# The first expert stage of a one-core hybrid kernel, split into three quarters and one quarter of the tokens

## Chip, core and metric

The kernel runs on one core of one Trainium2 chip. The metric is the device time of one execution in microseconds, as the median of several runs. TensorE (PE), VectorE (DVE), ScalarE (ACT) and GpSimd (POOL) each execute their own instructions in order and meet through semaphores; SyncE (SP) issues the transfers. A wait holds up everything that is queued behind it on its engine.

## What is computed

The input is 8 images of 64 channels and 16 x 16 pixels. Two convolution blocks are followed by four residual stages on 2048 tokens of 64 channels (`_ln_t` is a layer norm without weights):

```python
t = t + _L2_attn_ref(_ln_t(t), ...)   # softmax attention, 8 heads of 64
t = t + _L2_ffn_ref(_ln_t(t), ...)    # 8 experts, hidden 128, gelu, two chosen per token
t = t + _L3_attn_ref(_ln_t(t), ...)   # attention with a pseudo-inverse of W_Q as key weights
t = t + _L3_ffn_ref(_ln_t(t), ...)    # 16 experts, hidden 128, silu, two chosen per token
```

In `_L2_ffn_ref` the gates are a softmax over 8 logits of which the two largest per token are kept; every expert is computed for every token, its hidden layer is multiplied by the gate, and the outputs and gated biases are summed.

## The kernel before

**Stages.** The order is: convolutions, first norm, attention of L2, second norm with gates, first expert stage, third norm, attention of L3, fourth norm with gates, second expert stage. The 2048 tokens are 16 tiles of 128, or 4 chunks of 512. Attention round j (4 of them) covers images 2j and 2j+1, which are the 4 tiles of chunk j. `T` is the residual stream, `XS` the normalised stream turned to channels, split into a high part (rounded for the fast fp32r products) and the low rest.

**Attention.** A round has 8 pairs of heads. `attention_steps` (L335) runs each engine's `step(j, k)`, software-pipelined: four steps ahead, a hardware loop over rounds 0 to 2 with 8 steps each (k = 2 to 9), then the 8 steps of the last round written out. In one step DVE takes row maxima (`maxima`, L1574), splits keys (L1566), inverts row sums (L1581) and copies turned probabilities (L603); ACT does the exponentials (L619), key copies (L610), one turned copy (L601) and value copies; POOL scales the probabilities (`scale_rows`, L504) twice, for rows 2k+2 and 2k+3; PE makes scores (L857), keys (L833, L834), transposes (`turn`, L868), products (L884) and, every fourth step, `value` and `turn_out` (L895). `add_out` (L1589) adds a finished half round to `T`.

**Newton.** Inside the loop each step also has one Newton iteration for the pseudo-inverse: POOL makes `nsZ` (`newton_z`, L512) as its first instruction of the step; DVE makes `nsY` from it (`newton_y`, L1602) between the two maxima; PE uses `nsY` (L909, L910) after `turn(2k+1)`; DVE copies back (L1607). The order on DVE in a step is written out:

```python
maxima(j, 2 * k + 2)
newton_y(j, k - 2)          # in the loop; waits for POOL's nsZ
key_low(j, k + 2)
invert_sums(j, 2 * k + 2)
maxima(j, 2 * k + 3)        # then add_out in some steps
newton_x(j, k - 2)
transposed_copy(dve, j, 2 * k + 1)
invert_sums(j, 2 * k + 3)
```

**Second norm and gates.** After the attention, `layer_norm(1)` on DVE (L1504 statistics, L1508 to L1514 moments, L1522 scaling) works with POOL's centring of half the tiles (L462), ACT's square root (L574, with table loads), PE's transposes (L794), ACT's high parts (L369) and DVE's low parts (L377). `start_sums` (L954) puts the stream into the PSUM banks of the sums. `gate_pe` (L807) makes logits, `gate(0)` on DVE chooses (L1536 to L1542), ACT takes exponentials (L584) and loads the Gelu table (L586), DVE makes the gates (L1544 to L1549), PE turns them (L818) and ACT copies them into `gT` (L590). SP stores `gT` to HBM (L432) and loads it back as one row per expert, spread over 128 partitions (L441): 512 KB per half row, two per expert, in three buffers that are used in turn.

**First expert stage.** Items kk = 0 to 31 are (expert, chunk) with the chunk running fastest. PE makes a hidden item (L968, two fp32r matmuls of 512 columns), ACT the gelu (L725), DVE the multiplication by the gate row (L1650), PE the output matmul (`output`, L976, fp32, 64 output channels), which adds to one half of the partitions of bank 6 or 7: chunks 0 and 1 to the two halves of bank 6, chunks 2 and 3 to those of bank 7. A ring of 16 hidden items lies between; PE makes 16 hidden items, then 8 outputs, 8 hidden, 8 outputs, 8 hidden, 16 outputs. `biases` (L996) adds the gated biases. During the stage POOL splits the weights of the second expert stage into high and low parts (`split_weights`, L454 and L456, four experts at a time). ACT's copy of bank 6 (L741) ends the stage.

Of the kernel before, what the change touches and what calls it, by code (L numbers as in the profile page):

```python
# [21 lines left out]
F32 = mybir.dt.float32  # L22
# [6 lines left out]
P = 128  # L29
# [11 lines left out]
RING, GROUP = 16, 8  # L41
CT = CHUNK // P
# [7 lines left out]
NEWTON = (J - 1) * PAIRS  # L50
HIDDEN_SCORE = -30000.0
# [89 lines left out]
def hybrid_kernel(nc, io, out):  # L141
    ctx = ExitStack()
    with ctx:
# [33 lines left out]
        def from_early(rows, words):  # L177
# [65 lines left out]
                  for s in range(2))  # L243
# [43 lines left out]
                     over(at_keys, "gate_row_keys", [P, TOK])[:]]  # L287
        hid_more = sb("hid_more", [P, 2, CHUNK])
# [41 lines left out]
        def gate_slot(which, e):  # L330

            so_far = sum(f % 3 == e % 3 for f in range(EXP2)) if which == 3 else 0
            return e % 3, so_far + e // 3 + 1

        def attention_steps(eng, step, in_loop=None):  # L335
# [13 lines left out]
            for k in range(2, 2 + PAIRS):  # L349
                step(J - 1, k, lambda pair: pair < PAIRS)  # L350

# [12 lines left out]

        def split_high(act, stack, bank, p, signal):
# [6 lines left out]
        def split_low(dve, stack, bank, p, high, so_far, signal):  # L372

            for odd in range(2):
                h, o = slice(C * odd, C * odd + C), slice(C * (1 - odd), C * (1 - odd) + C)
                dve.wait_ge(S(high), so_far + 2 * p + odd + 1)
# [9 lines left out]
        def _(sp):  # L386
# [42 lines left out]
            for which, experts, rows in ((2, EXP2, gates_row2), (3, EXP3, gates_row3)):  # L429
                sp.wait_ge(S("gT_ready"), 2 * (which - 1))  # L430
                for o in range(2):
                    sp.dma_start(rows.rearrange("e (q o n) -> o e q n", o=2, n=P)[o],  # L432
                                 gT[C * o:C * o + experts]).then_inc(S("gates_stored"), 16)
                sp.wait_ge(S("gates_stored"), 32 * (which - 1))
                for e in range(experts):
                    slot, _ = gate_slot(which, e)
                    if e >= 3:
                        sp.wait_ge(S(f"f{which}_hid_ready"), CHUNKS * (e - 2))
                    for half in range(2):
                        at = slice(half * TOK // 2, (half + 1) * TOK // 2)  # L440
                        sp.dma_start(gate_rows[slot][:, at], rows[e:e + 1, at].broadcast_to([P, TOK // 2])).then_inc(  # L441
                            S(f"gate_row{slot}_{half}"), 16)
# [16 lines left out]
        def ln_pool(gp, n):  # L459

            gp.wait_ge(S("ln_mean"), n + 1)
# [37 lines left out]
        def attention_pool(gp):  # L499
# [14 lines left out]

            def step(j, k, there):
                if not isinstance(j, int):
                    newton_z(j, k - 2)
                if there(k + 1):
                    scale_rows(j, 2 * k + 2)
                    scale_rows(j, 2 * k + 3)  # L520

            gp.wait_ge(S("consts_loaded"), 16)
            attention_steps(gp, step)

        @block.gpsimd
        def _(gp):
# [5 lines left out]
            gp.memset(zeros[:], 0.0).then_inc(S("zeros_ready"), 1)  # L532
            gp.wait_ge(S("zeros_ready"), 1)
# [8 lines left out]
            gp.wait_ge(S("ln_normalised"), 4)  # L542
# [5 lines left out]
            ln_pool(gp, 1)  # L548
            gp.wait_ge(S("gates_ready"), 1)
            split_weights(gp, w3hl, w3raw, [slice(e, e + 4) for e in range(0, EXP3, 4)], "w3_loaded", "w3_high", "w3_split")  # L550
            ln_pool(gp, 2)
            l3_pool(gp)
            ln_pool(gp, 3)

            for kk in range(CHUNKS * EXP3):
                e, c = kk // CHUNKS, kk % CHUNKS
                slot, filled = gate_slot(3, e)
                gp.wait_ge(S(f"gate_row{slot}_{c // 2}"), 16 * filled)
# [12 lines left out]
        def ln_act(act, n, table_after=None):  # L571

            act.wait_ge(S("ln_var"), n + 1)
            act.activation(lnc[:, 6, :], lnc[:, 5, :], ACT.Sqrt).then_inc(S("ln_std"), 1)  # L574
            if table_after:
                act.preload_act_table(table_after)
            for p in range(4):
                act.wait_ge(S("ln_transposed"), 4 * n + p + 1)
                split_high(act, XS, p, p, "ln_high")
# [1176 lines left out]
```

## Time and profile before

| | us |
|---|---|
| median of 3 runs (lowest, highest) | 418.89 (418.32, 419.47) |
| the profiled execution | 416.06 |
| its span, first to last instruction | 414.3 |
| granted TensorE clock, mean over the span | 0.897 of full speed |
| busy: PE, DVE, ACT, POOL | 350.9, 283.2, 217.5, 189.2 |

Times inside the profile count from the start of the span. The attention loop runs to about 182, its last round to 206.9, the norm and gates to 218.4, and the first expert stage to about 262. A row of the timeline shows start, duration, engine, line and operation; "x8" means that eight such instructions are merged, and the bracket gives the engine's idle time just before and who ended it.

### The profile page before, as it was taken

To read this page: it belongs to the slowest core of one execution; us is meant where nothing else is said; L and a number is where in the kernel's file an instruction comes from. 1 tells how busy PE (TensorE), PEld (TensorE's weight loads), DVE (VectorE), ACT (ScalarE), POOL (GpSimd) and SP (SyncE) were. 2 spreads that over 40 slices of the span, in tenths; PEclk is the share of its full clock that TensorE was granted. 3 is DMA by queue.
4 is the path that set the end of the run, shared out by engine and by line. 5 is a ranking of instruction groups with operands and counts; after the bars stand their busy time and mean duration, and the time that the engine had idled before them with its cause. 6 is when DMAs were issued, how large, how long until landed. Compare 5 with 4: busy or idle time off the path is not lost.

```text
span 414.3 us, 6910 instructions
## 1 busy us (share of the span) xinstructions
PE 350.9 (85%) x2145; PEld 246.1 (59%) x2147; DVE 283.2 (68%) x689; ACT 217.5 (52%) x541; POOL 189.2 (46%) x186
## 2 busy tenths in 40 slices
PE   5666259999999999999769699877258999999996
PEld 1552156787888878887467244374147756666662
DVE  2767876788878878877493587579798545555441
ACT  0534258677677767778547435261315634444441
POOL 4120025545454545545315800122110299999994
PEclk9867559999999999999977789968556999999999
DMA  6916000000000000000000795000000576666521
GB/s 185 235 21 205 0 0 1 2 2 2 2 0 0 0 0 0 0 0 2 1 2 5 288 329 197 2 0 2 1 0 2 193 273 215 222 208 224 204 101 52
DMA packets 17002, 32.87 MB, mean 79 GB/s; under 512 B 6032, under 2 KB 9808, under 8 KB 16976
## 3 DMA queue, kind: packets, MB, share of 16 engines
q1 hardware_dynamic: 16976, 32.55, 23.9%
q8 instruction: 13, 0.21, 0.2%
q14 instruction: 13, 0.11, 0.1%
HBM read 31.83 MB, written 0.72 MB: 79 GB/s over the span
## 4 chain that ended last, share of the span: by engine, by line
PE 61%; DVE 19%; ACT 9%; issue 6%; DMA 3%; POOL 1%; SPq 0%; DVEq 0%; ACTq 0%; POOLq 0%
PE ps L1020 14%; PE ps L1028 7%; PE ps L857 6%; PE ps L884 5%; PE ps L868 5%; PE ps L976 4%; ACT va_vb L619 4%; DVE ln L1504 2%; DVE negmax L1574 2%; PE ps L968 2%; PE ps L807 2%; DMA pT<-gates_row 1%; PE ps L910 1%; PE ps L834 1%; PE ps L833 1%
## 5 line engine op out<-in xcount | busy, mean ns | idle before, releaser
L504 POOL TENSOR_TENSOR va_vb<-va_vb,rowinv 128x512 f32<-128x512 f32 x64 | 67.2, 1050 | 72.1 <-DVE rowinv L1581 72.1
L619 ACT ACTIVATE va_vb<-ps,negmax 128x256 f32<-128x256 f32 x128 | 59.5, 472 | 11.2 <-DVE negmax L1574 10.9
L1020 PE MATMUL ps<-XS,w3hl 128*128 128x512 f32 x256 | 63.4, 406 | 0.7 <-ACT gT L590 0.7
L733 ACT ACTIVATE wy<-ps 128x512 f32<-128x512 f32 x64 | 38.2, 598 | 45.6 <-PE ps L1020 45.6
L1020 PEld LDWEIGHTS ps<-XS,w3hl 128*128 128x128 f32 x256 | 48.6, 193 | 17.2 <-issue 4.9
L1574 DVE TENSOR_REDUCE negmax<-ps 128x2 f32<-128x512 f32 x64 | 44.0, 688 | 7.8 <-PE ps L857 5.6
L857 PE MATMUL ps<-keys_gates,xcur 128*128 128x256 f32 x256 | 47.4, 308 | 2.2 <-DVE keys_gates L1566 2.2
L857 PEld LDWEIGHTS ps<-keys_gates,xcur 128*128 128x128 f32 x256 | 35.1, 193 | 14.8 <-issue 11.5
L868 PE MATMUL ps<-consts,va_vb 128*128 128x128 f32 x256 | 39.5, 277 | 4.2 <-POOL va_vb L504 2.4
L462 POOL TENSOR_TENSOR xn<-T,lnc 128x512 f32<-128x512 f32 x4 | 4.2, 1042 | 74.0 <-DVE lnc L1512 74.0
L868 PEld LDWEIGHTS ps<-consts,va_vb 128*128 128x128 f32 x256 | 29.7, 147 | 9.8 <-POOL va_vb L504 4.8
L884 PE MATMUL ps<-pT,vproj 128*64 128x256 f32 x256 | 34.5, 392 | 0.0
L610 ACT ACTIVATE keys_gates<-ps 128x512 fp32r<-128x512 f32 x32 | 19.2, 600 | 25.8 <-PE ps L834 25.5
L619 ACT ACTIVATION_READ_ACCUMULATOR va_vb<-ps,negmax 128x1 f32 x128 | 25.7, 201 | 0.0
L603 DVE COPY pT<-ps 128x512 f32<-128x512 f32 x32 | 21.8, 681 | 1.9 <-PE ps L868 1.9
L1566 DVE TENSOR_TENSOR keys_gates<-ps,keys_gates 128x512 fp32r<-128x512 f32 x32 | 21.8, 683 | 1.4 <-ACT keys_gates L610 1.4
L1667 DVE TENSOR_TENSOR theta_qk<-ps,wy 128x512 f32<-128x512 f32 x16 | 11.1, 692 | 15.3 <-ACT wy L733 15.3
L884 PEld LDWEIGHTS ps<-pT,vproj 128*64 128x64 f32 x256 | 15.6, 136 | 8.9 <-issue 1.4
L601 ACT ACTIVATE pT<-ps 128x512 f32<-128x512 f32 x32 | 19.2, 601 | 0.2 <-PE ps L868 0.2
L1581 DVE RECIPROCAL rowinv<-rowsum 128x2 f32<-128x2 f32 x64 | 10.6, 165 | 12.7 <-ACT va_vb L619 10.7
L968 PE MATMUL ps<-XS,w2hl 128*128 128x512 f32 x64 | 18.6, 444 | 0.2 <-ACT x L725 0.2
L833 PE MATMUL ps<-xcur,AH 128*128 128x256 f32 x64 | 17.4, 293 | 0.5 <-DVE xcur L1559 0.5
(323 smaller groups left out, 727.9 us busy)
## 6 DMA issues: line engine op xcount, KB each, us to landing
pT<-gates_row SPq DMA_DIRECT2D x18, 512.0 KB, 4.8
vproj<-gates_row SPq DMA_DIRECT2D x16, 512.0 KB, 5.4
gate_row_keys<-gates_row SPq DMA_DIRECT2D x14, 512.0 KB, 4.9
early<-in_f_in SPq DMA_DIRECT2D x1, 2048.0 KB, 8.8
consts<-in_consts SPq DMA_DIRECT2D x1, 816.0 KB, 4.9
x<-in_x SPq DMA_DIRECT2D x1, 512.0 KB, 3.7
w2raw<-in_f_in SPq DMA_DIRECT2D x1, 512.0 KB, 3.5
out<-in_f_out SPq DMA_DIRECT2D x1, 512.0 KB
```

The costliest lines, as they stand in the source:

```text
L504: gp.tensor_tensor(prob[:, n % 4], prob[:, n % 4], rowinv[:, n % 4, :].unsqueeze(2).broadcast_to([P, U, N]), ALU.mult).then_inc(S("p_scale ...
L603: eng.tensor_copy(dst, src).then_inc(S("pT_odd"), 1)
L619: ins = act.activation(prob[:, n % 4, u, :], ps[:, 1 + n % 2, u * N:(u + 1) * N], ACT.Exp, bias=negmax[:, n % 4, u:u + 1], accum_out=rowsu ...
L733: act.activation(act_out[:, kk % 2, :], ps[:, 2 * (kk % 3), :], ACT.Silu).then_inc(S("f3_act"), 1)
L857: mm = pe.matmul(ps[:, 1 + n % 2, u * N:(u + 1) * N], xcur[:, g, u * P:(u + 1) * P], K[:, k % 2, n % 2, :], start=(part == 0), stop=(part ...
L868: mm = pe.transpose(ps[:, 3 + n % 2, su * N + u * P:su * N + (u + 1) * P], prob[:, n % 4, u, su * P:(su + 1) * P], ident)
L884: mm = pe.matmul(ps[h * C:(h + 1) * C, 5, 0:N], vproj[:, g, su, head * C:(head + 1) * C], pT[:, (2 * k + h) % 4, su, :], start=(k % 4 == 0 ...
L968: mm = pe.matmul(ps[:, kk % 4, :], w2hl[:, s, e], XS[:, c * CHUNK:(c + 1) * CHUNK], start=(s == 0), stop=(s == 1))
L1020: mm = pe.matmul(ps[:, 2 * (kk % 3) + w, :], w3hl[:, s, e, w * HID:(w + 1) * HID], XS[:, c * CHUNK:(c + 1) * CHUNK], start=(s == 0), stop= ...
L1028: pe.matmul(ps[half, bank, :], out3[:, e, :], hid[kk % RING], start=False, stop=False, skip_group_check=True).then_inc(S("f3_out_chunk"), 1)
L1566: tt(KL[:, k % 2].rearrange("p h n -> p (h n)"), ps[:, 0, :], KH[:, k % 2].rearrange("p h n -> p (h n)").bitcast(F32), ALU.subtract).then_ ...
L1574: dve.tensor_reduce(negmax[:, n % 4, :], ps[:, 1 + n % 2, :].rearrange("p (u n) -> p u n", u=U), AX.X, ALU.max, negate=True).then_inc(S("m ...
```

## The change

Layer norm n = 1 covers chunks 0 to 2 and is done in pieces behind the steps of the last attention round; a new norm n = 2 covers chunk 3 and is done inside the first expert stage. The norms are numbered 0 to 4 from here on. Cut to its core:

```diff
+NORMS = [(0, 1, 2, 3), (0, 1, 2), (3,), (0, 1, 2, 3), (0, 1, 2, 3)]
+SPLIT_A_ROUND = EXP3 // (J - 1)
+early_chunks = [(e, c) for e in range(EXP2) for c in NORMS[1]]
+first_experts = early_chunks + [(e, c) for e in range(EXP2) for c in NORMS[2]]
 def attention_steps(eng, step, in_loop=None, behind=lambda k: None):
             for k in range(2, 2 + PAIRS):
                 step(J - 1, k, lambda pair: pair < PAIRS)
+                behind(k)
```

POOL, attention (256 elements a partition are split for one expert; `split_weights` of w3 and `ln_pool(1)` behind the attention are gone):

```diff
             def step(j, k, there):
...
                     newton_z(j, k - 2)
+                i = k - 4
+                so_far = j * SPLIT_A_ROUND + i if in_loop else EXP3 - 1
+                splits = (in_loop and 0 <= i < SPLIT_A_ROUND) or (not in_loop and j == J - 1 and k == 2)
                 if there(k + 1):
                     scale_rows(j, 2 * k + 2)
+                    if splits:
+                        split_high_of(expert)
+                        gp.wait_ge(S("w3_high"), so_far + 1)
                     scale_rows(j, 2 * k + 3)
+                    if splits:
+                        split_low_of(expert)
```

Behind the steps of the last round, on DVE, ACT and PE (on PE `between(k)` stands inside the step, ahead of `turn(2k+1)`):

```diff
+                if k == 2:                                   # DVE
+                    split_pinv()
+                    dve.wait_ge(S("stream_added"), G + G * (J - 1))
+                    stats(1)
+                if k == 3:
+                    moments(1)
+                    centre(1, NORMS[1])
+                if k == 4:
+                    scale(1)
+                if k in (5, 6, 7):
+                    low(1, k - 5, 6)
+                if k == 9:
+                    choose(0, EXP2, gb2, [(tiles_of_norm(1), 6, 0)])
...
+                if k == 3:                                   # ACT
+                    ln_root(act, 1, ACT.Exp)
+                if k in (5, 6, 7):
+                    ln_highs(act, 1, lambda i: 6, (k - 5,))
+                if k == 9:
+                    gate_exp(act, 0, EXP2, tiles_of_norm(1))
...
+            def between(k):                                  # PE
+                if k == 2: pinv product
+                if k in (5, 6, 7):
+                    pe.wait_ge(S("ln_low"), chunks_before(1) + k - 5)
+                    ln_turn(pe, 1, k - 5, 6)
+            def behind(k):
+                if k == 8:
+                    pe.wait_ge(S("ln_low"), chunks_before(2))
+                    gate_products(pe, 1, range(0, 12), 6, EXP2, gw2)
```

After the attention. DVE: `share_out(0)`, then stats, moments, centre, scale and low parts of norm 2, `weigh(0)`, `weigh(1)`, `choose(1)`, `weigh(2)`, `weigh(3)`, `share_out(1)`, `weigh(4)` and on. ACT and PE:

```diff
+            turned_gates(act, slice(0, 4), 4, 0)
+            turned_gates(act, slice(4, 6), 6, 1)
+            ln_root(act, 2, ACT.Gelu)
+            gelu 0, 1
+            ln_highs(act, 2, lambda i: 4, (0,))
+            gelu 2 to 7
+            gate_exp(act, 1, EXP2, tiles_of_norm(2), ACT.Gelu)
+            gelu 8 to 11
+            turned_gates(act, slice(6, 8), 4, 2)
+            gelu 12 and on
...
+            gates_turn(pe, range(0, 4), 4); gates_turn(pe, range(4, 6), 6)
+            hidden 0 to 3, ln_turn(pe, 2, 0, 4), start_sums, hidden 4 to 7
+            gate_products(pe, 2, range(12, 16), 5, EXP2, gw2)
+            biases(NORMS[1], 0), hidden 8 to 15
             for k in range(0, CHUNKS * EXP2, GROUP):
                 for kk in range(k, k + GROUP):
                     output(kk)
+                    if kk == 1:
+                        pe.wait_ge(S("gates_ready"), 2)
+                        gates_turn(pe, range(6, 8), 4)
+                if k + RING == len(early_chunks):
+                    pe.wait_ge(S("gT_ready"), 3)
+                    biases(NORMS[2], 1)
```

SP now loads a gate row in pieces of one chunk (256 KB each). The 24 early pieces have blocks of their own (`row_blocks`), so none waits for another; the 8 late ones reuse the first blocks:

```diff
+            sp.wait_ge(S("gT_ready"), 2)
+            store_gates(gates_row2, EXP2, slice(0, 6), 0)
+            for e in range(EXP2):
+                if e == 3:
+                    sp.wait_ge(S("pv_done"), PAIRS + J * PAIRS)
+                for c in NORMS[1]:
+                    first_row(early_row(e, c), e, c, f"first_gates{e}")
+            sp.wait_ge(S("gT_ready"), 3)
+            store_gates(gates_row2, EXP2, slice(6, 8), 32)
+            for e in range(EXP2):
+                sp.wait_ge(S("f2_hid_ready"), len(NORMS[1]) * (e + 1))
+                first_row(late_row(e), e, NORMS[2][0], f"first_gates{e}")
```

The item order of the first expert stage becomes chunks 0, 1, 2 of each expert (24 items), then chunk 3 of each (8 items). The later stages keep their work; only semaphore counts change there.

## Rows read from the trace of the kernel before

**Rows 1.** Stretches: us, busy (count) of PE, PEld, DVE, ACT, POOL; PE clock, DMA share, GB/s.
```profile
145.50:182.30 36.80, 36.29 (x291) 29.94 (x290) 29.79 (x69) 26.89 (x86) 18.96 (x25) 1.00 0.00 0
182.30:206.90 24.60, 22.28 (x170) 16.54 (x169) 14.69 (x32) 17.91 (x55) 11.16 (x11) 1.00 0.01 1
...
218.40:232.80 14.40, 11.97 (x43) 7.95 (x41) 3.47 (x17) 11.94 (x20) 10.74 (x7) 0.83 0.20 71
232.80:262.60 29.80, 28.63 (x114) 11.86 (x114) 21.77 (x32) 10.07 (x17) 3.50 (x2) 0.89 0.69 250
```

**Rows 2.** Timeline of one step of the attention loop, DVE and POOL.
```profile
169.88 0.35 DVE L1602 SCALAR_TENSOR_TENSOR nsY<-ps,nscoef,nsZ 128x128 f32<-128x128 f32 x1 [0.60 <-POOL nsZ L512]
...
172.58 0.17 DVE L1581 RECIPROCAL rowinv<-rowsum 128x2 f32<-128x2 f32 x1
...
172.82 1.04 POOL L504 TENSOR_TENSOR va_vb<-va_vb,rowinv 128x512 f32<-128x512 f32 x1 [0.80 <-DVE rowinv L1581]
...
173.82 0.29 POOL L512 TENSOR_TENSOR nsZ<-consts,nscoef 128x64 f32<-128x64 f32 x1
...
174.15 0.35 DVE L1602 SCALAR_TENSOR_TENSOR nsY<-ps,nscoef,nsZ 128x128 f32<-128x128 f32 x1 [0.26 <-POOL nsZ L512]
```

**Rows 3.** Timeline of DVE: newton_y in steps k = 4 and k = 9 of that round.
```profile
156.29 0.35 DVE L1602 SCALAR_TENSOR_TENSOR nsY<-ps,nscoef,nsZ 128x128 f32<-128x128 f32 x1 [0.35 <-POOL nsZ L512]
...
178.83 0.35 DVE L1602 SCALAR_TENSOR_TENSOR nsY<-ps,nscoef,nsZ 128x128 f32<-128x128 f32 x1 [0.35 <-POOL nsZ L512]
```

**Rows 4.** Waits, 112 to 145: engine, for whom, us in total, times, longest.
```profile
DVE nsY L1602 <- POOL nsZ L512: 2.9, 7, 0.7
```

**Rows 5.** POOL's groups by shape: busy, mean ns, then idle before.
```profile
L560 POOL TENSOR_TENSOR theta_qk<-theta_qk,gate_row_keys 128x512 f32<-128x512 f32 x8 | 10.1, 1304 | 0.4 <-DVE theta_qk L1667 0.4
...
L456 POOL TENSOR_TENSOR w3hl<-early,w3hl 128x1024 fp32r<-128x1024 f32 x4 | 9.8, 2450 | 0.3
...
L454 POOL CAST w3hl<-early 128x1024 fp32r<-128x1024 f32 x4 | 4.6, 1157 | 10.3 <-DVE gates L1549 10.3
```

**Rows 6.** Timeline of the last round's end: the last copy of turned probabilities.
```profile
203.53 0.69 DVE L603 COPY pT<-ps 128x512 f32<-128x512 f32 x1 [1.87 <-PE ps L868]
```

**Rows 7.** Timeline of the second norm and the gates.
```profile
207.41 2.11 DVE L1504 BATCH_NORM_STATS2 ln<-T 128x6 f32<-128x64 f32 x16
...
207.64 2.54 PE L954 MATMUL ps<-consts,T 128*64 128x128 f32 x32 [0.74 <-DVE qkvw L1639]
...
211.77 1.28 ACT L576 ACT_TABLE_LOAD   x1
...
212.42 1.43 DVE L1522 TENSOR_TENSOR xn<-xn,lnc 128x256 f32<-128x256 f32 x4
...
213.88 3.52 DVE L377 TENSOR_TENSOR XS<-ps,XS 64x256 fp32r<-64x256 f32 x8
...
214.88 3.60 PE L807 MATMUL ps<-gw,XS 128*64 128x8 f32 x64
...
217.69 0.64 DVE L1539 MAX8 top<-logit 128x8 f32<-128x8 f32 x8
```

**Rows 8.** Timeline of the first expert stage: store of the gates, first gated item, end.
```profile
225.23 1.56 SPq L432 DMA_DIRECT2D gates_row<-gT  x2
...
231.90 2.28 DVE L1650 TENSOR_TENSOR hid_al<-hid_al,pT 128x512 f32<-128x512 f32 x2 [10.15 <-DMA pT<-gates_row]
...
261.72 0.60 ACT L741 ACTIVATE x<-ps 128x512 f32<-128x512 f32 x1 [4.71 <-PE ps L976]
```

**Rows 9.** Timeline of PE: hidden and output items at full clock; a full-width fp32 product.
```profile
243.99 3.99 PE L968 MATMUL ps<-XS,w2hl 128*128 128x512 f32 x16
...
258.90 1.89 PE L976 MATMUL ps<-theta_qk,out 128*64 128x512 f32 x8
...
285.24 1.88 PE L1068 MATMUL ps<-f_prob,consts 128*128 128x512 f32 x4
```

**Rows 10.** A stretch of the expert stage: PE clock, DMA share and GB/s come last.
```profile
244.00:248.00 4.00, 4.00 (x20) 2.93 (x20) 3.17 (x6) 3.23 (x6) 0.00 (x0) 1.00 1.03 372
```

More of the change, by code:

```diff
@@ L330, in gate_slot, with early_row, late_row, attention_steps @@
         def gate_slot(which, e):
-            so_far = sum(f % 3 == e % 3 for f in range(EXP2)) if which == 3 else 0
-            return e % 3, so_far + e // 3 + 1
-        def attention_steps(eng, step, in_loop=None):
+            return e % 3, e // 3 + 1
+        def early_row(e, c):
+            return row_blocks[len(NORMS[1]) * e + c]
+        def late_row(e):
+            return row_blocks[e]
+        def attention_steps(eng, step, in_loop=None, behind=lambda k: None):
             for k in range(-2, 2):
@@ L823, in attention_pe, with gates_turn @@
+        def gates_turn(pe, pairs, bank):
+            for t in pairs:
+                at = (t - pairs[0]) * P
+                mm = pe.transpose(ps[:, bank, at:at + P], gates[:, 2 * t:2 * t + 2].rearrange("p t c -> p (t c)"), ident)
+            mm.then_inc(S("gates_transposed"), 1)
         def attention_pe(pe):
@@ L936, in step @@
                     upto(pe, "nsy_ready", j, PAIRS, k)
+                if not in_loop and j == J - 1:
+                    between(k)
                 if there(k):
@@ L1216, in _ @@
             start_sums(pe)
-            ln_pe(pe, 3)
-            gate_pe(pe, 1)
+            ln_pe(pe, 4)
+            for half in range(2):
+                gate_products(pe, 4, range(8 * half, 8 * half + 8), 4 + half, EXP3, gw3)
             ffn3_pe(pe)
@@ new lines, in centre, with scale @@
+            def centre(n, chunks):
+                for p in chunks:
+                    q = slice(CT * p, CT * p + CT)
+                    ins = tt(xn[:, q], T[:, q], wide(lnc[:, 1, q], t=CT), ALU.subtract)
+                step(ins)
+            def scale(n):
+                tiles = tiles_of_norm(n)
+                dve.wait_ge(S("ln_std"), n + 1)
+                step(dve.reciprocal(lnc[:, 7, tiles], lnc[:, 6, tiles]))
+                for p in NORMS[n]:
+                    q = slice(CT * p, CT * p + CT)
+                    if p == 2 and n in WHOLE:
+                        dve.wait_ge(S("ln_centred"), WHOLE.index(n) + 1)
+                    tt(xn[:, q], xn[:, q], wide(lnc[:, 7, q], t=CT), ALU.mult).then_inc(S("ln_normalised"), 1)
@@ new lines, in choose @@
+                tiles = slice(parts[0][0].start, parts[-1][0].stop)
+                count = tiles.stop - tiles.start
+                lg, gs = logit[:, tiles, 0:experts], gsel[:, tiles, 0:experts]
+                for k, (piece, bank, so_far) in enumerate(parts):
+                    dve.wait_ge(S("gate_logits"), so_far + 1)
+                    t = piece.stop - piece.start
+                    raw = ps[:, bank, 0:t * experts].rearrange("p (t e) -> p t e", e=experts)
+                    step(tt(logit[:, piece, 0:experts], raw, gb[:].unsqueeze(1).broadcast_to([P, t, experts]), ALU.add))
+                    for q in range(piece.start, piece.stop):
+                        ins = dve.max(top8[:, q, :], logit[:, q, 0:experts])
@@ L1652, in _ @@
+            stats(2)
+            moments(2)
+            centre(2, NORMS[2])
+            scale(2)
+            low(2, 0, 4)
+            for kk in range(2):
+                weigh(kk)
+            choose(1, EXP2, gb2, [(tiles_of_norm(2), 5, 1)])
+            for kk in range(2, 4):
+                weigh(kk)
+            share_out(1, EXP2, tiles_of_norm(2))
+            for kk in range(4, CHUNKS * EXP2):
+                weigh(kk)
             dve.wait_ge(S("f2_out_chunk"), CHUNKS * EXP2)
```

328 lines of the change are left out of this document (179 added, 149 removed).

## The prediction

> **What bounds the kernel now.** I read the stretches first [rows 1], to see which engine is short where. In a loop round (36.8 us, [rows 1]) PE is busy for 36.3, so it looks like the bound; POOL is busy for 19.0 and looks half free. In the last round PE is at 22.3 of 24.6 and DVE and ACT have 9.9 and 6.7 us idle. From 207.4 to 218.5 the norm and the logits run one after another [rows 7], and up to 232.8 DVE has almost nothing to do: it waits for the first gate row, which starts as a store at 225.23 and lets DVE go at 231.90 [rows 8]. From there to 261.72 PE is the bound again (28.6 busy in 29.8, [rows 1]). So the idle stretch between 206.9 and 231.9 is what the change goes for.
>
> Busy shares don't show a second bound in the loop. I read the waits [rows 4]: in every one of seven steps DVE waits for POOL's nsZ ahead of newton_y. One step [rows 2] shows the ring: newton_y at 169.88; DVE then works its queue down to the second reciprocal at 172.58 (2.70); POOL scales at 172.82; nsZ follows at 173.82 in the same queue; newton_y again at 174.15 (1.57). That is 4.27 us, the shortest step of the round. From step 4 to step 9 newton_y comes every (178.83 - 156.29) / 5 = 4.51 us [rows 3], and each time DVE has stood waiting for nsZ. PE's own pace is 36.3 / 8 = 4.5 us a step. Ring and PE are equally long.
>
> **The loop: 15 splits.** In steps k = 4 to 8 of each round POOL gets a cast and a subtraction of 256 elements. The subtraction takes 2.45 us at 1024 elements, a like one (two full operands) 1.30 at 512 [rows 5]: the slope is 1.15 / 512, so 256 elements cost 1.30 - 0.57 = 0.73, and about 0.78 if I take the undisturbed part of the slope; I take 0.78. The cast takes 1.16 at 1024 [rows 5], I estimate 0.35 at 256. It and its semaphore wait stand between the two scalings, where POOL idles for 0.80 [rows 2], so they cost nothing; without that gap they would cost 0.4 each. The subtraction stands behind the second scaling and ahead of the next step's nsZ, that is, in the ring. Everything behind newton_y on DVE (key split, reciprocals, second maximum, PSUM copy) waits for it, and with those ACT's exponentials, POOL's scaling and PE's transposes.
>
> A ring with it is at least 2.70 + 1.57 + 0.78 = 5.05 and at most 4.51 + 0.78 = 5.29 against the 4.51 of just these five steps now [rows 3]. Fifteen times 0.54 is 8.1, fifteen times 0.78 is 11.7, with some 0.8 on top for register work on the expert's address. No row shows an instruction with such an address on POOL. I take **+10 us**, bounds 8 and 12.5. The sixteenth split, in step 2 of the last round, has no nsZ behind it and is free.
>
> **The last round.** Each insertion is queued behind a step and ahead of the next step's first maximum (DVE) or key copy (ACT).
> - k = 2: the inverse's split, about 0.5, and 12 statistics, 12/16 of 2.11 [rows 7] = 1.6. DVE +2.1.
> - k = 3: moments, about 1.1 (an estimate: 2.25 lie between the end of the statistics and the table load at 211.77, [rows 7], with POOL's centring of 1.04 and the root of 0.2 among them), and three centrings at 1.43 / 4 = 0.36. DVE +2.2. ACT has two table loads of 1.28 and a root of 0.2: +2.8. The longer counts, and ACT's key copy is late next.
> - k = 4: reciprocal and three scalings, 1.35.
> - k = 5, 6, 7: per chunk two low parts of 0.44 [rows 7] on DVE and two high parts of about 0.4 on ACT, 0.9 and 0.8, side by side, shifted by one part; PE's transposes 0.5. PE's wait for the low parts of the chunk before stands ahead of turn(2k+1), where it holds up the products once the round is short of work. About 0.9, 0.4 and 0.3.
>
> The sum is 2.1 + 2.8 + 1.35 + 1.6 = 7.9. The idle time of the round absorbs little, since DVE's gaps are waits for ACT's exponentials and for PE, which move along. I take **+7.5** at the last copy of turned probabilities (203.53, [rows 6], to 211.0); bounds +3 (DVE's 14.7 us plus 9.5 of insertions just fit into 24.6) and +9.
>
> **From there to the first gated item.** Products follow the copy and now end at about 213. Ahead of turn_out PE has 48 of the 64 logit matmuls, 3.60 x 48/64 = 2.7 at half clock [rows 7], 1.5 at full: 214.9. Turn_out 0.5, add_out 0.3, choice of 12 tiles (12 x 0.08 from [rows 7], and three small ones, 1.8), exponential with latency 0.4, share_out 1.2, six transposes 1.2: hidden items start at 220.3, against 218.5 behind the logits [rows 7], later than now. But gT is ready at 221.1 instead of 225.23, since no norm and no Gelu table load is ahead. The same 6.7 us from store to first use [rows 8] and 0.6 for a third piece give the first gated item at **228.4 instead of 231.9**. That the rows come in pieces of 256 KB costs nothing as long as the DMA engines are full; 24 pieces, 6.3 MB at 372 GB/s [rows 10], land by about 243, ahead of the items.
>
> **From there to the end.** PE has 32 outputs (8 records in 1.72 us of spacing, so 0.43 an output, [rows 9]; 14), 16 hidden (3.92 for 8, [rows 9]; 7.8), bits of 1.0. That is 22.8. On top comes a new wait: behind output(1) PE waits for the second gates, which need ACT's exponential, queued behind gelu(7) and between two table loads of 1.28. ACT reaches it at about 231 and DVE shares out by 234: PE stands still for some 5 us, and weigh(4) and on with it. 228.4 + 22.8 + 5.2 = 256.4, against 262.4 now (261.72 with its last copy). The late rows queue behind the early ones on SP's ring and land by 252; the items want them then, so they cost 0 to 3. Also gone is POOL's splitting beside DVE's first multiplications (1.14 each in [rows 8], later ones about 0.65), which is in these numbers. Tail without the loop: **-6 us**, bounds -10 and -2.
>
> **The sum.** +10 - 6 = +4. The profiled execution's 416.06 becomes 420.1; it lies 2.8 below the median of the runs, so I put +4 on the median: 418.89 + 4 = **422.9**. Everything behind the stage is unchanged.
>
> **Rivals.**
> - *POOL's half-idle time covers the splits* (the side of faster). If nsZ has slack, the loop costs 1 us or less and the change gives 418.9 - 6 + 1 = 413.9. For it speaks POOL's 19.0 of 36.8 [rows 1]; against it [rows 2 to 4]: DVE stands waiting for nsZ in each step. It decides from where less than 0.4 of the 0.78 reaches newton_y. Chance 0.17.
> - *The order of the halves.* Outputs of 64 channels alternate between partition halves now. In the new order chunks 0, 2 and the next 0 share a half, and all eight late ones do. An fp32 product of full width needs 1.71 for four records of 512 columns, the 64-wide outputs 1.72 for eight [rows 9]: they may run two at a time because the halves differ. Then 8 pairs of records in the early part and 8 in the late part lose their partner, 16 x 0.43 = 6.9, and the time is 422.9 + 6.9 = 429.8. Against it: start_sums has eight records in a row on one half, and 32 of 128 columns take 2.54 [rows 7], 0.073 each; two cycles a column would be 0.107. So narrow fp32 products seem fast in either order, and the sum has nothing for it. The Trainium skill ("TensorE: Matmul & The Clock Gate", Part 3, packing small matmuls) says that small products run concurrently when they lie in distinct column groups, which is this rival's rule; by it the sum would be 429.8, and the start_sums row speaks against needing it. Chance 0.12.
> - *The tail pays for the loop.* The last round takes the insertions for +4 or the second gates cost no stall, while the loop is as forecast: tail -10, result 418.9. DVE's 9.9 idle us [rows 1] speak for it; that they are waits in a chain speaks against. Chance 0.14.
> - Forecast: 0.57.
>
> **The numbers.** 0.3% (1.26 us) is about what a measurement of this kernel can tell from no change. Forecast with its bounds: loop 8 to 12.5, tail -8 to -3, so 418.9 to 428.4, its own range. The range 414.5 to 430 reaches to the tail case and the halves and leaves the covered case mostly out. Slower: 0.52 + 0.12 + 0.03 = 0.67; same: 0.04 + 0.06 = 0.10; faster: 0.17 + 0.01 + 0.05 = 0.23.
>
> **What the profile will show.** Loop rounds of 40 us instead of 36.8, with DVE's wait for nsZ at 1 us or more in five of eight steps and PE no longer full; if rounds stay at 36.8, the ring was read wrongly. A last round of about 32 instead of 24.6, the root's table loads in its middle. First gated item 3.5 us earlier relative to the loop's end; PE waiting 5 us behind output(1). Outputs still at 0.43 each; at 0.6 or more in the early part, the halves decide.

## Result and profile after

| | before | after |
|---|---|---|
| median, us (lowest, highest) | 419.18 (418.32, 419.5) | 427.92 (426.92, 428.83) |
| profiled execution; span | 416.06; 414.3 | 427.19; 425.4 |
| last nsZ of the loop starts | 178.50 | 186.99 |
| last scaling of POOL starts | 201.74 | 217.91 |
| first gated item starts | 231.90 | 235.95 |
| statistics of the norm behind the first expert stage start | 264.74 | 275.10 |

The change makes the kernel slower by 8.7 us between the medians (a ratio of 1.021); the ratio of all its runs to those of before is on record as 1.0225, with a 95% interval of 1.0192 to 1.0259. The forecast was 4 us slower. (The median of before has one run more behind it here than in the table ahead of the prediction.) The two profiled executions are 11.1 us apart, because that of before lies 3.1 under its median and that of after only 0.7; 10.4 of these are there at the end of the first expert stage, which the next norm's statistics mark. I follow the time from one milestone to the next.

**The loop.** The page of after has a new kind of entry in its part 4, the chain that ended last: POOL's split of the late weights.

```profile
PE 41%; issue 21%; DVE 18%; POOL 9%; ACT 8%; DMA 1%; POOLq 1%; DVEq 0%; ACTq 0%; SPq 0%
PE ps L1138 12%; PE ps L1146 6%; PE ps L1085 5%; PE ps L1077 4%; ACT va_vb L689 3%; POOL va_vb L553 3%; POOL w3hl L568 3%; DVE ln L1622 2%; DVE negmax L1722 2%; DVE XS L406 2%; POOL nsZ L561 2%; POOL w3hl L565 1%; PE ps L1231 1%; PE ps L903 1%; DVE xn L1654 1%
```

POOL's timeline shows one step of it (L553 scales, L565 is the cast to the high part, L568 the subtraction that gives the low part, L561 nsZ):

```profile
144.16 1.04 POOL L553 TENSOR_TENSOR va_vb<-va_vb,rowinv 128x512 f32<-128x512 f32 x1 [1.13 <-DVE rowinv L1729]
145.15 0.40 POOL L565 CAST w3hl<-early  x1
146.01 1.13 POOL L553 TENSOR_TENSOR va_vb<-va_vb,rowinv 128x512 f32<-128x512 f32 x1 [0.46 <-DVE rowinv L1729]
147.10 0.74 POOL L568 TENSOR_TENSOR w3hl<-early,w3hl  x1
147.79 0.30 POOL L561 TENSOR_TENSOR nsZ<-consts,nscoef 128x64 f32<-128x64 f32 x1
```

nsZ starts at 142.73 and again at 147.79: 5.06 us for a step with a split. The subtraction stands between the second scaling and nsZ, and nsZ is what DVE waits for. The waits of DVE from 112 to 152 (for whom, us in total, times, longest) say the same, against 2.9 us in 7 times before [rows 4]:

```profile
DVE nsY L1750 <- POOL nsZ L561: 6.3, 7, 1.1
```

From the first nsZ to the last the loop now takes 112.5 us (74.50 to 186.99), where it took 104.9 (73.63 to 178.50). So the loop costs 7.6; the other 0.9 of the difference in the table is there before the first nsZ. Profiles of kernels that are the same up to that point put it anywhere from 73.6 to 75.7.

**The stretches** (columns as in [rows 1]): a piece of the loop, of the last round, the start of the expert items, and their end.

```profile
110.00:150.00 40.00, 38.03 (x296) 30.50 (x297) 29.69 (x72) 27.19 (x87) 24.84 (x35) 1.00 0.00 0
190.00:214.00 24.00, 19.39 (x136) 14.17 (x135) 19.07 (x56) 16.64 (x48) 10.29 (x11) 1.00 0.00 1
234.00:246.00 12.00, 11.94 (x71) 6.70 (x68) 9.50 (x25) 9.63 (x16) 0.00 (x0) 1.00 1.02 366
254.00:273.00 19.00, 18.94 (x66) 7.73 (x65) 6.39 (x12) 5.62 (x10) 0.00 (x0) 1.00 0.52 96
```

In these 24 us of the last round DVE is busy for 19.1, where it was at 14.7 of 24.6 [rows 1]: the insertions are there, and from the last nsZ to POOL's last scaling the round gets longer by 7.7 ((217.91 - 201.74) - (186.99 - 178.50)). In the last two rows PE hardly pauses and its granted clock is full; before, the stage had 0.89 [rows 1]. A stage with PE full at full clock that is still longer must have more PE time in it. The chain of waits shows where (start, us, what; PE is the chain all the way):

```profile
228.72 3.27 PE ps L1077 x8
...
232.20 2.50 PE ps L1063 x32
234.70 2.04 PE ps L1077 x8
236.74 0.57 PE ps L903 x16
237.31 1.02 PE ps L1096 x6
...
238.37 1.07 PE ps L1096 x6
239.45 4.44 PE ps L1077 x16
243.89 1.01 PE ps L1085 x4
244.90 0.37 PE ps L910 x2
245.27 3.58 PE ps L1085 x12
248.85 3.91 PE ps L1077 x16
252.76 5.29 PE ps L1085 x16
...
259.32 3.92 PE ps L1077 x16
263.25 9.66 PE ps L1085 x32
```

L1085 is the output product, two records for each. 32 records took 9.66 us here. In before's chain of waits the same piece is 7.07 long:

```profile
255.49 7.07 PE ps L976 x32
```

All 64 records together: 1.01 + 3.58 + 5.29 + 9.66 = 19.5 us, where 64 at the spacing of 1.72 / 8 [rows 9] would be 13.8. The first gated item starts at 235.95, the first output only at 243.82, with PE busy all the time between on what the new order put ahead of it: the rest of the hidden items 4 to 7 (L1077), the logits of the last tiles (L903), the gated biases (L1096), and the hidden items 8 to 15.

### The profile page after: what moved, and what is told of

It is laid out like the page before. It is cut to its first block, busy times and chain, and to the rows that moved or that the text cites. A ratio compares the mean times of both kernels' runs of the same rounds, so it can differ in the third digit from the quotient of the medians.

```text
span 425.4 us, 7015 instructions
## 1 busy us (share of the span) xinstructions
PE 356.6 (84%) x2147; PEld 245.4 (58%) x2147; DVE 280.9 (66%) x706; ACT 222.0 (52%) x547; POOL 190.0 (45%) x208
## 3 DMA queue, kind: packets, MB, share of 16 engines
q1 hardware_dynamic: 19296, 32.56, 24.6%
## 4 chain that ended last, share of the span: by engine, by line
PE 41%; issue 21%; DVE 18%; POOL 9%; ACT 8%; DMA 1%; POOLq 1%; DVEq 0%; ACTq 0%; SPq 0%
PE ps L1138 12%; PE ps L1146 6%; PE ps L1085 5%; PE ps L1077 4%; ACT va_vb L689 3%; POOL va_vb L553 3%; POOL w3hl L568 3%; DVE ln L1622 2%; DVE negmax L1722 2%; DVE XS L406 2%; POOL nsZ L561 2%; POOL w3hl L565 1%; PE ps L1231 1%; PE ps L903 1%; DVE xn L1654 1%
## 5 line engine op out<-in xcount | busy, mean ns | idle before, releaser
L553 POOL TENSOR_TENSOR va_vb<-va_vb,rowinv 128x512 f32<-128x512 f32 x64 | 67.2, 1050 | 70.9 <-DVE rowinv L1729 70.9
L511 POOL TENSOR_TENSOR xn<-T,lnc 128x512 f32<-128x512 f32 x3 | 3.1, 1042 | 94.3 <-DVE lnc L1632 94.3
L958 PEld LDWEIGHTS ps<-consts,va_vb 128*128 128x128 f32 x256 | 28.8, 146 | 17.2 <-DVE nsY L1750 11.5
L1850 DVE TENSOR_TENSOR theta_qk<-ps,wy 128x512 f32<-128x512 f32 x16 | 11.1, 692 | 15.3 <-ACT wy L810 15.3
L1750 DVE SCALAR_TENSOR_TENSOR nsY<-ps,nscoef,nsZ 128x128 f32<-128x128 f32 x24 | 8.4, 350 | 19.0 <-POOL nsZ L561 19.0
L1729 DVE RECIPROCAL rowinv<-rowsum 128x2 f32<-128x2 f32 x64 | 10.4, 163 | 12.6 <-ACT va_vb L689 11.8
L1077 PE MATMUL ps<-XS,w2hl 128*128 128x512 f32 x64 | 18.2, 437 | 0.0
```

The lines of the kernel that those rows point to most:

```text
L553: gp.tensor_tensor(prob[:, n % 4], prob[:, n % 4], rowinv[:, n % 4, :].unsqueeze(2).broadcast_to([P, U, N]), ALU.mult).then_inc(S("p_scale ...
L958: mm = pe.transpose(ps[:, 3 + n % 2, su * N + u * P:su * N + (u + 1) * P], prob[:, n % 4, u, su * P:(su + 1) * P], ident)
L1077: mm = pe.matmul(ps[:, kk % 4, :], w2hl[:, s, e], XS[:, c * CHUNK:(c + 1) * CHUNK], start=(s == 0), stop=(s == 1))
```

## Experiments

Four theories were left. **Ring**: the place of the subtraction costs the loop's part. **Halves**: outputs on one partition half in a row cost double. **Late rows**, against the second: the late gate rows set the end. **Table loads**: ACT's table loads cost what the last round lost.

### 1. The low split behind nsZ

```diff
                 if in_loop:
                     newton_z(j, k - 2)
+                if in_loop and 1 <= k - 4 <= SPLIT_A_ROUND:
+                    split_low_of(bass.ds(j * SPLIT_A_ROUND + k - 5, 1))
...
                     scale_rows(j, 2 * k + 3)
-                    if splits:
+                    if splits and not in_loop:
                         split_low_of(expert)
```

> The changed kernel, with the same 16 splits and one edit: in the loop the subtraction of an expert's low part stands behind the next step's nsZ instead of ahead of it. Ring theory (newton_y waits for nsZ, which waits for POOL's queue): steps go back from 5.0 to about 4.5 us, a loop round from 39.2 to about 36.8, the whole from 427.9 to about 420. Rival, the amount of POOL's work slows the loop (contention with DVE, more instructions), wherever it stands: rounds stay at 39.2 and the time at 427.9.

Measured: 420.96 us (418.76 to 421.81), ratio to before 1.0033 (1.001 to 1.0056), so 7.0 below after, as the ring theory expected. The last nsZ starts at 179.33 instead of 186.99, and from the first to the last there are 105.0 us, the 104.9 of before. POOL's timeline and DVE's wait from 108 to 145:

```profile
136.89 1.04 POOL L553 TENSOR_TENSOR va_vb<-va_vb,rowinv 128x512 f32<-128x512 f32 x1 [0.46 <-DVE rowinv L1731]
137.89 0.29 POOL L561 TENSOR_TENSOR nsZ<-consts,nscoef 128x64 f32<-128x64 f32 x1
138.14 0.74 POOL L568 TENSOR_TENSOR w3hl<-early,w3hl  x1
```

```profile
DVE nsY L1752 <- POOL nsZ L561: 2.9, 7, 0.7
```

The same fifteen splits, on the same engine, now cost the loop nothing: the wait is back at the 2.9 of before [rows 4]. From one nsZ to the next it is 142.56 - 137.89 = 4.67 here, against 5.06. The ring theory holds. It was never POOL's load, only what stood ahead of nsZ.

### 2. The items with alternating halves, alone and with experiment 1

```diff
-        first_experts = early_chunks + [(e, c) for e in range(EXP2) for c in NORMS[2]]
+        first_experts = [(e, c) for e in range(EXP2) for c in (0, 1)] + [(e, c) for e in range(EXP2) for c in (2, 3)]
```

SP's order of rows, their semaphores and two of the buffers follow.

> The changed kernel, with the first expert stage in another order of items: first chunks 0 and 1 of all experts, then chunks 2 and 3 of all, so that every output product lies on the other half of the partitions than the one before. Halves theory: an output costs 0.43 us instead of 0.43 to 0.86, the stage ends about 6.9 us earlier, 421.0. Rival, the late rows of chunk 3 set the end (they land at a lower rate than the early ones): the stage ends no earlier, since those rows come no earlier; 427 to 429.

> Both edits together. Ring and halves theories: the gains add, 427.9 - 8 - 6.9 = about 413, below the kernel before (419.2) by 6, which is the return of the earlier first gated item less the cost of the last round. If the two share a cause, they don't add: 420 or more.

Measured: 431.06 us (430.94 to 431.27), 3.1 above after; with experiment 1 423.84 (422.19 to 425.75), 2.9 above experiment 1 alone. Both expectations of a gain fail, and the total is even above the range of the rival, late rows (427 to 429). The timeline of PE shows both why it should have held and what took its place:

```profile
253.19 1.94 PE L1086 MATMUL ps<-theta_qk,out 128*64 128x512 f32 x8
254.96 1.89 PE L1086 MATMUL ps<-probT_rot,out 128*64 128x512 f32 x8
...
263.97 1.67 PE L1086 MATMUL ps<-hid_al,out 128*64 128x512 f32 x4 [1.95 <-DVE hid_al L1823]
265.67 1.67 PE L1086 MATMUL ps<-hid_g,out 128*64 128x512 f32 x4
```

The alternating outputs are back at 8 records in 1.77 us. The last sixteen, four records in 1.67, wait for the multiplication, and that waits for its gate row. Behind 264 the DMA engines are full and move little (last two columns, share and GB/s). The single rows also start late: the store of the second gates, which they need, takes 6.8 us to land behind the rows that are already under way (252.72 to 259.5 in the chain of waits; the first store took 1.6).

```profile
252.00:256.00 4.00, 4.00 (x20) 1.67 (x20) 0.00 (x0) 2.77 (x5) 0.00 (x0) 1.00 0.59 170
...
268.00:273.00 5.00, 4.92 (x14) 1.24 (x14) 3.88 (x6) 0.00 (x0) 0.00 (x0) 1.00 0.99 159
```

That is 159 GB/s at a share of 0.99, where [rows 10] has 372 at 1.03. Rows of a single chunk, one for each expert, lie 8 KB apart in DRAM. Whether that is the reason stayed open until experiment 7.

### 3. Before, with its chunks in the order 0, 2, 1, 3

```diff
-                e, c = kk // CHUNKS, kk % CHUNKS
+                e, c = kk // CHUNKS, (0, 2, 1, 3)[kk % CHUNKS]
```

The same in hidden, output and DVE's multiplication; ACT's last copy waits for one output more. The halves then come as 0, 0, 1, 1.

> The kernel before, with chunks of an expert in the order 0, 2, 1, 3, so that the halves of the partitions come as 0, 0, 1, 1 instead of 0, 1, 0, 1; everything else is the same. Halves theory: of 8 records of 4 outputs only two pairs overlap, 6 x 0.43 instead of 4 x 0.43 us, +0.86 for each of 8 experts: +6.9 less what is hidden early in the stage, 424 to 426. If narrow fp32 products run at the same rate in any order: 419.2.

Measured: 417.77 us (416.56 to 421.69), ratio 0.9987 (0.9953 to 1.0022): no difference. Its four runs at a mean clock of 0.89 or less, where most of before's are, take 420.7 to 421.7 against before's 418.8 to 420.9, so a small cost isn't excluded; the expected 5 to 7 us are. I had expected a loss, and this miss corrected the theory. The timeline of PE at the start of the last sixteen outputs, of which the first two read hid_al (one half) and the next two hid_g (the other); I call these four items 0 to 3:

```profile
257.39 0.64 PE L976 MATMUL ps<-hid_al,out 128*64 128x512 f32 x1
257.40 0.64 PE L976 MATMUL ps<-hid_g,out 128*64 128x512 f32 x1
257.87 0.59 PE L976 MATMUL ps<-hid_al,out 128*64 128x512 f32 x1
257.88 0.59 PE L976 MATMUL ps<-hid_g,out 128*64 128x512 f32 x1
```

Item 2's first record starts 0.01 us behind item 0's first and 0.47 ahead of item 0's second. PE fetched it past the second record of item 0 and all of item 1, which stand ahead of it in the program. (The text ahead of the prediction says that each engine executes its instructions in order; for these products of PE that doesn't hold.) The Trainium skill ("TensorE: Matmul & The Clock Gate", Part 3) calls matmuls strictly first in, first out; for products on different halves these starts say otherwise, and the measurement decides. So, within what PE can look ahead, what counts is not who is whose neighbour but how many outputs of a stretch lie on either half. In after these are 5 and 3, 6 and 2, and in the last sixteen 5 and 11. With 0.86 us for each on the fuller half (twice the 0.432 of experiment 4) that makes 4.3, 5.2 and 9.5; the chain has 4.59, 5.29 and 9.66.

### 4. Narrow products by themselves

A kernel that only multiplies; all of the reference's work is left out. 16 products of each kind follow one another:

```diff
+            for k in range(16):   # halves alternate
+                pe.matmul(half(k % 2, 2, 512), w(k, C), x0[:, 0:512], ...)
+            for k in range(16):   # one half
+                pe.matmul(half(0, 3, 512), w(k, C), x0[:, 0:512], ...)
+            for k in range(16):   # full width
+                pe.matmul(ps[:, 4, :], w(k, P), x0[:, 0:512], ...)
```

and the same at 256 and 128 columns, and with four on one half, then four on the other, as `start_sums` has them.

> Only products, in groups of 16 with nothing between: all the reference's work is left out. Spacing of the records tells how narrow fp32 products run. Halves theory: 64 output channels, 512 columns, alternating halves 0.21 us a record; the same half 0.43; full width 0.43. At 128 columns on the same half 0.11 would follow, where start_sums showed 0.073: if 128 columns on the same half come out at 0.07, the cost depends on the columns in another way than two cycles each.

```profile
17.65 7.09 PE L194 MATMUL ps<-x 128*64 128x512 f32 x32
24.56 13.90 PE L196 MATMUL ps<-x 128*64 128x512 f32 x32
38.39 14.00 PE L198 MATMUL ps<-x 128*128 128x512 f32 x32
...
67.97 3.66 PE L208 MATMUL ps<-consts,x 128*64 128x128 f32 x32
71.47 2.52 PE L210 MATMUL ps<-consts,x 128*64 128x128 f32 x32
73.91 3.84 PE L212 MATMUL ps<-x 128*128 128x128 f32 x32
```

The granted clock is full in all of these. From start to start, 512 columns cost 6.91 / 32 = 0.216 us a record on alternating halves (L194), 13.83 / 32 = 0.432 on one half (L196) and 0.435 at full width (L198). A product of half the width on one half saves nothing. At 128 columns one half costs 3.50 / 32 = 0.109 (L208), and four and four 2.44 / 32 = 0.076 (L210). The last is close to the number that my prediction read off `start_sums` (0.073) and took for the price of one half. It was the price of two halves at a time. The halves theory holds at 128 columns too.

### 5. Before, with only the splits moved into the loop, as the change has them and with the low split behind nsZ

```diff
+SPLIT_A_ROUND = EXP3 // (J - 1)
...
                     scale_rows(j, 2 * k + 2)
+                    if splits:
+                        split_high_of(expert)
+                        gp.wait_ge(S("w3_high"), so_far + 1)
                     scale_rows(j, 2 * k + 3)
+                    if splits:
+                        split_low_of(expert)
...
-            split_weights(gp, w3hl, w3raw, [slice(e, e + 4) for e in range(0, EXP3, 4)], "w3_loaded", "w3_high", "w3_split")
```

> The kernel before, with the splits of the second expert stage's weights moved into the attention loop as the change has them, and nothing else. Ring theory: the loop costs the 8 us that the changed kernel shows. Behind it POOL no longer splits beside DVE's first gated items, which gives back 1 to 2. Sum +6 to +8: 425 to 427. If the splits cost nothing in the loop: 417 to 418.

> The kernel of e5_before_loop_splits (before, with the splits of the last stage's weights moved into the attention loop) with one edit: the low split stands behind the next step's nsZ, as in e1. e5 took 421.42 with its last nsZ at 187.0 and the later stages about 6 us shorter than before's. If the ring theory holds here as in e1, the last nsZ falls to about 179.3 and the time to 421.4 - 7.0 = 414.4 (412.5 to 416.5), faster than before: then moving the splits is worth it, and only the place of the low split in POOL's step cost. If the time e5 got back later was won only because its attention came late (weights and rows waiting ready), it stays with the loop and the time is 418 to 420.

Measured: 421.42 us (419.89 to 425.39), ratio 1.0059 (1.0029 to 1.009), less than the 425 to 427 expected; with the low split behind nsZ 417.45 (414.38 to 420.26), ratio 0.9983 (0.9945 to 1.0021), not to be told from before and in neither of the two ranges expected. The last nsZ starts at 187.02 in the first, +8.5 as in after, and at 178.68 in the second. But the time falls by 4.0, or by 3.2 if each is taken against before on its own chip, and not by 7. From the first gated item to the next norm the first takes 29.7 us (241.2 to 270.9), the second 35.3 (232.3 to 267.5), and before 32.8. The granted clock is the third number from the end of these rows, which are first of the kernel with the low split behind nsZ, then of the other:

```profile
235.00:240.00 5.00, 4.17 (x13) 1.34 (x12) 4.74 (x8) 0.00 (x0) 0.00 (x0) 0.50 1.03 377
240.00:245.00 5.00, 4.93 (x18) 1.52 (x16) 4.08 (x7) 0.00 (x0) 0.00 (x0) 0.50 1.01 407
```

```profile
235.00:240.00 5.00, 3.93 (x14) 1.81 (x13) 0.00 (x0) 5.00 (x10) 0.00 (x0) 1.00 0.43 123
240.00:245.00 5.00, 3.09 (x7) 1.05 (x8) 3.04 (x5) 0.46 (x1) 0.00 (x0) 0.73 0.94 338
```

In the first pair PE multiplies its items at 0.50, that is at 1.2 GHz, for all of the ten microseconds; in the second mostly at 2.4 GHz, but its gated items only start at 241.2. Over the whole stage, from each kernel's first gated item to its next norm, the mean clock is 0.81 with the low split behind nsZ, 0.94 in the other, and 0.90 before. Part of what the late loop lost came back as clock. The runs say the same. At a mean clock of 0.91 over the whole kernel the first took 419.9 to 421.5, and the one run of the second at 0.909 took 414.4, about 7 less. The other nine runs of the second had 0.886 to 0.898 and took 415.9 to 420.3. (The profiled execution of the second is one of those, 2.6 above its median.) What moved the low stretch was not tested.

### 6. The insertions behind the last round; the root without table loads

The first moves every insertion of the last round behind it. The second takes a plain copy instead of the square root in norm 1, which leaves that root out, and its two table loads.

```diff
+            for k in range(2, 2 + PAIRS):
+                behind(k)
```

```diff
-            act.activation(lnc[:, 6, tiles], lnc[:, 5, tiles], ACT.Sqrt)
-            if table_after:
+            act.activation(lnc[:, 6, tiles], lnc[:, 5, tiles], ACT.Copy if n == 1 else ACT.Sqrt)
+            if table_after and n != 1:
```

> The changed kernel, with all pieces of norm 1, its turns, logits and choice done behind the last attention round instead of within it. If the insertions cost the last round 7.7 us and are cheap only because they lie within it, the round goes back to 24.6 us and the pieces then take about 12 us behind it in a row: +3 to +5, 431 to 433. If the pieces cost more within the round than behind it (each step waits for them on three engines): 427.9 or less.

> The changed kernel, with a copy in place of the square root of norm 1 and without its two table loads (the gates of the early tokens are thus other values; the work is the same otherwise). If ACT's two loads of 1.28 us in step 3 of the last round are on the path: -2 to -2.6 us, 425.5. If DVE's moments and centring beside them set that step: -0.6 at most.

Measured: 432.91 us (431.31 to 433.78) and 426.82 (425.79 to 427.9), so 5.0 above and 1.1 below after. The insertions are worth 5 us where the change put them, as expected. For the loads, 1.1 lies between the two expectations (2 to 2.6, or 0.6 at most), so I read the profiles. From the last nsZ to POOL's last scaling there are 216.67 - 186.06 = 30.61 us without the loads and 217.91 - 186.99 = 30.92 with them. The loads cost the round 0.3. Of the rest, 0.9 in these two profiles lies ahead of the last nsZ (186.06 and 186.99), where the two kernels are the same. So the table loads are not what makes the kernel slow, and DVE's share of the step alone fills nearly all of its place.

### 7. The gate rows 10 KB apart

One edit on three kernels: experiment 1 with 2, experiment 2 alone, and the changed kernel. The store writes the same 8 KB of each row as before.

```diff
-        gates_row2 = nc.dram_tensor("gates_row2", [EXP2, TOK], F32, kind="Internal").ap()
+        gates_row2 = nc.dram_tensor("gates_row2", [EXP2, TOK + CHUNK], F32, kind="Internal").ap()
```

> The kernel of e3_both (low split behind the next step's nsZ, and items with the halves alternating), with one edit: the rows of the first expert stage's gates in DRAM lie 10 KB apart instead of 8 KB (512 unused floats behind each). e3 took 423.84. Its single-chunk rows moved at some 160 GB/s with the DMA engines busy 0.9, against 372 to 400 GB/s for the rows of chunks 0 and 1. Theory A (the rate falls because all sources of one chunk lie at the same place modulo 8 KB): the rate rises towards 370, the outputs are no longer paced by rows but by PE at the alternating cost (32 x 0.43 = 14 instead of 19.4), time 423.84 - 5 = 418.8 (416 to 420.5). Theory B (the rate falls because of what else goes with one row for each expert, such as a DMA of one 2 KB source alone being slow): the rate stays at 160 and the time within 1 of 423.8.

> The kernel of e2_halves_alternate with the same edit of the pitch (rows of gates 10 KB apart in DRAM). e2 took 431.06. Theory A (source addresses): rows land in time, outputs at 0.43 for each product through all 32, time 427.9 - 5.3 = 422.6 (421 to 424.5), so that the halves' order alone is shown to be worth what after's same-half runs cost. Theory B (single rows are slow by themselves): within 1 of 431.1.

> The changed kernel with only the pitch of the gate rows changed (10 KB instead of 8 KB). In its trace the late rows went at some 160 GB/s too, but its last sixteen outputs took 9.6 us, which is eleven products running on one half at 0.86 each, and no row was waited for. So both theories expect 427.9 within 1; theory A also that the windows behind 251 show 300 GB/s or more, theory B 160. If the time falls by 3 or more, the late rows and not the halves set the changed kernel's end, and the tail's reading is wrong.

| | rows 8 KB apart | rows 10 KB apart |
|---|---|---|
| changed kernel | 427.92 | 427.39 (426.36 to 429.28) |
| halves alternate | 431.06 | 422.06 (421.08 to 423.13) |
| low split behind nsZ | 420.96 | not run |
| both | 423.84 | **415.08** (413.45 to 416.32) |

The pitch alone is worth 9.0 and 8.8 us where the halves alternate (8.3 and 8.1 if each is taken against before on its own chip), and nothing that shows in the changed kernel. The kernel with all three edits came out below the 416 to 420.5 expected of it. On the same chip 427.39 - 422.06 = 5.3 is the price of the halves, and 422.06 - 415.08 = 7.0 that of the split's place; the second is what experiment 1 gave. A stretch in which the late rows land, of after and then of the changed kernel with the new pitch:

```profile
256.00:260.00 4.00, 3.94 (x12) 1.44 (x11) 0.00 (x0) 0.00 (x0) 0.00 (x0) 1.00 0.77 162
```

```profile
256.00:260.00 4.00, 4.00 (x12) 1.15 (x10) 1.36 (x3) 0.40 (x1) 0.00 (x0) 1.00 0.91 290
```

162 GB/s become 290; in after no stretch of 4 us from 252 to 264 has more than 171. There the slow rows still came in time, since PE needed 0.86 for an output. The chain of waits of the kernel with all three edits has the outputs back at the old price:

```profile
236.66 1.01 PE ps L1088 x4
...
238.04 2.73 PE ps L1088 x12
...
244.67 3.58 PE ps L1088 x16
...
253.42 7.07 PE ps L1088 x32
```

That is 14.4 for all 64 records, against 19.5 in after: 5.1 less, nearly all of the 5.3. This kernel is faster than both before and after: ratio to before 0.992 (0.9891 to 0.9949), and 3.4 us below before's 418.51 on that chip.

## Why the prediction was wrong

The direction held, and so did the last round and the start of the gated items. The step that failed is the last one, from the first gated item to the end. It turned the tail, which is all that lies behind the loop, from a forecast gain of 6 us into a loss of 2. The loop came out 3 cheaper than forecast and hid part of that. In the forecast's own steps:

- **The loop, +10 (8 to 12.5).** The ring was read rightly, and the rival that POOL's idle time covers the splits falls: DVE waits 6.3 us in seven steps. The size was somewhat high. A step with a split takes 4.96 to 5.06, not 5.05 to 5.29; the subtraction measures 0.74 (0.78 taken, where the slope gave 0.73), the cast 0.40 (0.35). The 0.8 for register work had no row behind it, and these steps leave no room for it. A round takes 39.2 us where I had named 40. The loop itself gets longer by 7.6, and 7.0 of the time hang on the place of the subtraction (experiments 1 and 7); both are just below the lower bound.
- **The last round, +7.5 (3 to 9).** Measured +7.7. The term inside it that gave ACT's table loads the longer part of step 3 was 0.6 for them; they cost 0.3 (experiment 6).
- **The first gated item.** The forecast moved it 3.5 earlier, counted from the end of the loop. Measured: 235.95 - 186.99 = 48.96 against 231.90 - 178.50 = 53.40, so 4.4 earlier.
- **From there to the end, 28.0 us forecast.** The last output ends at 272.9, so it took 37.0. This is the step that failed, by 9.0, and it has three terms. (a) Outputs: 14 forecast, 19.5 measured. The halves were dismissed on the `start_sums` row, and that row was misread: its 0.073 a record belongs to a stretch of four on one half and four on the other, which PE runs at the same time (experiment 4). The term was 5.5 too small, and the pair of kernels in experiment 7 that differ in the order of the items shows 5.3 of it. The rival had put 6.9 on it, since it counted lost neighbours; the count on the fuller half is what decides (experiment 3). The rule of the Trainium skill that was cited there ("TensorE: Matmul & The Clock Gate", Part 3), that small matmuls in distinct column groups run at the same time, agrees with experiment 4; the reading of the trace against it was wrong. (b) The stall of 5.2 behind output(1). It did not appear: the turn of the second gates stands in the chain with 0.37 and no wait. In its place 7.9 us of PE work lie between the first gated item and the first output, for which the sum had nothing. Its sixteen hidden items behind the first gated one suppose that the first sixteen were made by then, but only about six were, and the logits of the last tiles and the biases stood ahead of the rest; that is 2.7 more than the stall. (c) Late biases and turn: 1.0 forecast, 1.6 measured.
- **The tail, -6 (-10 to -2).** Experiment 1 stands 1.8 above before with the loop's cost gone, so the tail was about +2 and outside its bounds. With the halves in order, and the rows far enough apart for that order, it is 415.08 - 418.51 = -3.4, inside them.
- **The sum.** 7.0 for the split's place, 5.3 for the halves and -3.4 for the rest make 8.9. These are differences between neighbours in a row of four kernels on one chip, so they add up to its whole by construction; that the whole is 8.9 there and 8.7 in the result shows only that the two chips agree. What the change was made for, the early gates, is worth having. It was paid for more than three times over by two things that the change brought with it.
- **Outputs still at 0.43 each; at 0.6 or more in the early part the halves decide.** This was the check I had named. The first sixteen came at (1.01 + 3.58 + 5.29) / 16 = 0.62, the last sixteen at 9.66 / 16 = 0.60.

## What to carry to other kernels

When work is put into an engine's idle time, put it behind the instruction of that engine that others wait for: the same split of 0.74 us cost 7 us ahead of nsZ and nothing behind it. When items are reordered, count for each stretch what the new order does to every resource that the old one shared out evenly by accident, here the two partition halves of the output and the addresses of the gate rows. And if a row is to dismiss a rival, look up in which order its instructions were issued.

## What the runs showed of the hardware

- An fp32 product with 64 output channels costs as much as one with 128 when its neighbours lie on the same partition half (0.432 and 0.435 us a record at 512 columns, experiment 4), and half of that when both halves have work (0.216). PE finds that work itself, from behind at least two products in program order (experiment 3).
- Transfers of a 2 KB piece to 128 partitions, the pieces 8 KB apart in DRAM, moved 159 GB/s with the DMA engines 0.99 busy (experiment 2); 10 KB apart they reached 290 at 0.91 (experiment 7). In after the early pieces, three neighbours for each expert, go at 398 GB/s from 244 to 248. That the addresses are the cause is shown by the one edit; which part of the memory they share is not.
- Two kernels whose loops end 8.3 us apart (experiment 5) end 4.0 apart: the later one had a mean clock of 0.94 in the next expert stage, the earlier one 0.81.
